# Router columns inside the first gate product, and the residual of the first layer added on TensorE

## The reference, cut to what matters

```python
x = x + xattn(ctx, layernorm(x), ...)   # selective scan over 512 positions, 16 states for each of 512 channels
x = x + ffn(layernorm(x), ...)          # router + 2 of 16 experts + one shared expert
# inside xattn, after the scan:
y = ys + D * u ; y = y * silu(z)        # z is the normalised x, turned to channels
# inside ffn:
logits = x @ gate_w.T                   # 16 router columns, softmax, top 2
gu_s = x @ shared_gate_up               # 4 * 352 columns: gate, then up
y = routed(x) + (silu(g) * u) @ shared_down
```

## Time and profile before

| | us |
|---|---|
| median of three runs (1036.51 to 1041.99) | 1039.0 |
| the profiled execution, its own time | 1039.41 |
| its span, first to last instruction | 1037.3 |
| outside the span in that execution | 2.1 |
| PE busy | 902.5 |
| DVE busy | 823.2 |
| POOL busy | 745.5 |
| ACT busy | 529.9 |
| mean granted TensorE clock, share of 2.4 GHz | 0.922 |

### The profile page before, as it was taken

One profiled execution on the slowest core, in us unless ns is written; L12 is line 12 of the kernel. 1 busy time (PEld: TensorE's weight loads), 2 busy tenths in 40 slices (PEclk: granted clock), 3 DMA queues, 4 the chain that ended last, 5 costly groups with the idle time before them and its releaser, 6 DMA issues.

```text
span 1037.3 us, 16660 instructions
## 1 busy us (share of the span) xinstructions
PE 902.5 (87%) x4352; PEld 658.6 (63%) x4353; DVE 823.2 (79%) x1348; ACT 529.9 (51%) x997; POOL 745.5 (72%) x465
## 2 busy tenths in 40 slices
PE   6787556779999889988999999889998999998994
PEld 2233245556666556655666565659988999897993
DVE  5788899999999799989999616766999979898000
ACT  3767734446665566655665322135544555454551
POOL 1436699889999899989993101148877888887873
PEclk9878765689999999999999989989998999999997
DMA  6467922563228422562210410254767767684433
GB/s 208 147 246 286 371 79 87 198 238 91 72 73 305 162 81 81 208 234 85 81 61 31 147 59 11 70 175 123 227 164 211 181 173 226 159 245 91 79 61 41
DMA packets 70260, 152.14 MB, mean 147 GB/s; under 512 B 7602, under 2 KB 24498, under 8 KB 64579
## 3 DMA queue, kind: packets, MB, share of 16 engines
q1 hardware_dynamic: 59682, 126.97, 35.3%
q0 software_dynamic: 10528, 24.65, 12.1%
HBM read 112.80 MB, written 38.80 MB: 146 GB/s over the span
## 4 chain that ended last, share of the span: by engine, by line
PE 45%; DVE 27%; issue 16%; DMA 5%; ACT 2%; POOL 2%; DVEq 1%; SPq 1%; POOLq 0%; ACTq 0%
DVE bank L1415 7%; PE bank L790 6%; PE bank L792 6%; PE bank L791 6%; PE bank L686 6%; PE bank L705 6%; DVE gs L1429 6%; PE bank L632 4%; PE bank L561 2%; DVE e_gu_lo L1578 2%; DVE e_gu_hi L1577 1%; PE bank L779 1%; DVE h_p L1415 1%; DMA xt<-x_scratch 1%; DVE p_acc L1355 1%
## 5 line engine op out<-in xcount | busy, mean ns | idle before, releaser
L1221 POOL TENSOR_TENSOR dbu<-bcs,m_w 128x2048 f32<-128x2048 f32 x64 | 296.5, 4634 | 21.4 <-DMA u_scratch<-p_u 8.5
L966 ACT ACTIVATE bank<-m_dt,c_a 128x512 f32<-128x512 f32 x256 | 171.7, 686 | 173.3 <-DVE gs L1429 173.2
L1415 DVE TENSOR_TENSOR_SCAN bank<-bank,dbu 128x512 f32<-128x512 f32 x192 | 229.9, 1217 | 11.3 <-ACT bank L966 7.4
L686 PE MATMUL bank<-ws_gu,f_xnT 128*128 128x352 f32 x576 | 192.7, 476 | 1.9 <-ACT f_hT L988 1.7
L632 PE MATMUL bank<-ident,gs 128*128 128x128 f32 x768 | 134.5, 307 | 54.8 <-DVE gs L1429 47.6
L632 PEld LDWEIGHTS bank<-ident,gs 128*128 128x128 f32 x768 | 97.9, 156 | 110.1 <-DVE gs L1429 89.1
L686 PEld LDWEIGHTS bank<-ws_gu,f_xnT 128*128 128x128 f32 x576 | 107.1, 197 | 49.4 <-issue 6.1
L790 PE MATMUL bank<-e_gu_hi,e_xT_hi 128*128 x376 | 130.0, 346 | 6.5 <-POOL e_xT_lo L1283 3.1
L1429 DVE TENSOR_TENSOR gs<-bank,bcs 128x512 f32<-128x512 f32 x192 | 127.3, 670 | 0.0
L792 PE MATMUL bank<-e_gu_hi,e_xT_lo 128*128 x376 | 122.0, 324 | 0.0
L791 PE MATMUL bank<-e_gu_lo,e_xT_hi 128*128 x376 | 121.8, 324 | 0.0
(11 more groups left out here) (175 smaller groups left out, 1692.2 us busy)
## 6 DMA issues: line engine op xcount, KB each, us to landing
bcs<-bc_scratch SPq DMA_DIRECT2D x32, 1024.0 KB, 9.1
e_gu<-in_wgu SPq DMA_DIRECT2D x16, 1408.0 KB, 9.0
e_dn<-in_wdn SPq DMA_DIRECT2D x16, 512.0 KB, 4.3
out_rows<-xt SPq DMA_DIRECT2D x18, 256.0 KB, 2.1
p_x<-in_x SPq DMA_DIRECT2D x4, 1024.0 KB, 6.8
u_scratch<-p_u SPq DMA_DIRECT2D x4, 1024.0 KB, 4.3
silu_z_scratch<-p_sz SPq DMA_DIRECT2D x4, 1024.0 KB, 5.6
dt_scratch<-p_dt SPq DMA_DIRECT2D x4, 1024.0 KB, 4.6
```

What stands on the lines that cost most here:

```text
L686: last = mm(dst[:, 0:I], lhs[t], ws_gu[:, t, off:off + I], start=t == 0, stop=t == KH - 1)
L966: f(HS[k % RING_H][:], m_dt[:, q % 2, :], ACT.Exp, scale=c_a[:, q, n:n + 1]).then_inc(exp_done, 1)
L1221: g.tensor_tensor(part_, Bs[:, gr * GRP:(gr + 1) * GRP, :], w, ALU.mult).then_inc(dbu_ready, 1)
L1415: v.tensor_tensor_scan(to, h, dbu[:, n, :], 0.0, ALU.mult, ALU.add).then_inc(scan_done, 1)
```

## The change

- `ws_gu` gets 16 more columns between the first 352 (gate, first half) and the rest, and the router's weights are loaded there; the tile `c_gate` is gone as a tile of its own. The load at L414 becomes three transfers, and one of the transfers at L371 is gone. In the slots 4 to 15, and for two tiles in the tail, the first gate product is 368 columns wide instead of 352, and ScalarE copies the 16 logits from its bank. The `router` product stays for three tiles in the tail, now one behind the other after the fourth `xn_turn`.
- `take_y` writes the gated rows to SBUF (in place of silu(z)) instead of PSUM. In slots 1 to 15 TensorE then adds them and x in bank 7 by two products with the unit matrix, 512 columns each, after the second `y_sum` of the slot; ScalarE copies the bank to `m_x` at n = 6, ahead of `gate`, and this increments `x1_ready`. `gated` on VectorE stays only once, after the last slot.

```diff
-        c_gate = sb("c_gate", [P, KH, NE])
-        ws_gu = sb("ws_gu", [P, KH, 4 * I])
+        ws_gu = sb("ws_gu", [P, KH, 4 * I + NE])
+        c_gate = ws_gu[:, :, I:I + NE]
...
+ADD_X_AT, X1_AT = 1, 6
-TAKE_AT, LOGITS_AT, GATED_AT, HIDDEN_AT, STATS_AT, ADD_AT = 2, 5, 4, (9, 13), (8, 1), 15
+TAKE_AT, LOGITS_AT, HIDDEN_AT, STATS_AT, ADD_AT = 2, 5, (9, 13), (8, 1), 15
...
+            def add_x(b, i, q, copied):
+                pe.wait_ge(y_taken, i + 1)
+                pe.wait_ge(x_loaded[q % 2], b * 32 + (q // 2) * 16 + 16)
+                pe.wait_ge(xnT_copied, 1 + copied)
+                mm(TP[:], ident[:], m_szT[:, q % 2, :], start=True, stop=False)
+                mm(TP[:], ident[:], m_x[:, q % 2].rearrange("p t j -> p (t j)"), start=False, stop=True).then_inc(x_added, 1)
...
                     dst, off, done = GU[c], half * 2 * I + c * I, (gate_ready, up_ready)[half]
+                    off += NE if off else 0
+                    wide = I + NE if with_logits and off == 0 else I
...
                             pe.wait_ge(sg_ready, 2 * f[0] + c + 1)
+                            if with_logits and c == 0:
+                                pe.wait_ge(lg_copied, 1 + f[0])
                         for t in ts:
-                            last = mm(dst[:, 0:I], lhs[t], ws_gu[:, t, off:off + I], start=t == 0, stop=t == KH - 1)
+                            last = mm(dst[:, 0:wide], lhs[t], ws_gu[:, t, off:off + wide], start=t == 0, stop=t == KH - 1)
...
-                if rows:
-                    router(f, f[0], f[0])
                 for piece in early[0:PE_AT[0]] + late[0:LATE_AT[0]]:
                     piece()
                 for n in range(NS):
                     y_sum(b, q, n)
+                    if n == ADD_X_AT and not (isinstance(i, int) and i == 0):
+                        add_x(*((b, i - 1, q - 1) if q else (b - 1, i - 1, DT - 1)), i - DT if rows else 0)
...
-            whole((first + 1, 1), first)
+            whole((first + 1, 1), None, with_logits=True)
             for q in range(TB - 1):
                 xn_turn((first + q, q), B * DT)
-                router((first + q, q), first + q + 1, first + 2)
-            whole((first + 2, 2), NT - 1)
+            whole((first + 2, 2), None, with_logits=True)
             xn_turn((NT - 1, TB - 1), B * DT)
-            router((NT - 1, TB - 1), NT, NT - 1)
-            router((NT, 0), NT, NT - 1)
+            for f in range(NT - 2, NT + 1):
+                router((f, f % TB), NT - 1)
...
+            def x1_copy(b, i, q):
+                act.wait_ge(x_added, i + 1)
+                f(m_x[:, q % 2], TP[:].rearrange("p (t j) -> p t j", t=TB), ACT.Copy).then_inc(x1_ready, 1)
...
             def lg_copy(fx):
-                act.wait_ge(lg_ready, fx[0] + 1)
-                f(logits[:, bass.ds(fx[0], 1), :].rearrange("p a e -> p (a e)"), LG, ACT.Copy).then_inc(lg_copied, 1)
+                act.wait_ge(gate_ready, 2 * (fx[0] + 1) + 1)
+                f(logits[:, bass.ds(fx[0], 1), :].rearrange("p a e -> p (a e)"), LOGITS, ACT.Copy).then_inc(lg_copied, 1)
...
                     if n == DU_AT:
                         skip(b, q)
+                    if n == X1_AT and not first:
+                        x1_copy(*((b, b * DT + q - 1, q - 1) if q else (b - 1, b * DT - 1, DT - 1)))
...
-            def take_y(b, i, q, copied):
+            def take_y(b, i, q, to):
                 dve.wait_ge(ymm_done, (i + 1) * NS)
-                dve.wait_ge(xnT_copied, 1 + copied)
                 dve.wait_ge(s_loaded[q % 2], b * 32 + (q // 2) * 16 + 16)
-                v.tensor_tensor(TP[:], Y[:], m_szT[:, q % 2, :], ALU.mult).then_inc(y_taken, 1)
+                v.tensor_tensor(to, Y[:], m_szT[:, q % 2, :], ALU.mult).then_inc(y_taken, 1)
...
                     if n == TAKE_AT and later:
-                        take_y(*((b, i - 1, q - 1) if q else (b - 1, i - 1, DT - 1)), i - DT if rows else 0)
-                    if n == GATED_AT and later:
-                        gated(*((b, i - 1, q - 1) if q else (b - 1, i - 1, DT - 1)))
+                        take_y(*((b, i - 1, q - 1) if q else (b - 1, i - 1, DT - 1)), m_szT[:, (q + 1) % 2, :])
```

More of the change, by code:

```diff
@@ L98, in program @@
         G, U = GU
-        LG = YO[:, 0:NE]
+        LG, LOGITS = YO[:, 0:NE], GU[0][:, I:I + NE]
         RANK, TOT, TABLE = bank[0], bank[3], bank[7]
@@ L264, in program @@
             gx0_loaded gx1_loaded ex_ready exT_copied eg_ready eu_ready esg_ready eh_ready ehT_ready ehT_copied
-            ey_ready ey_taken scattered tstat_done route_step idx_step waits_passed row_scaled norm_made in_rest moment_done""".split()
+            ey_ready ey_taken scattered tstat_done route_step idx_step waits_passed row_scaled norm_made in_rest moment_done x_added""".split()
         s = {n: sem(n) for n in names}
@@ L294, in program @@
         moment_done = s["moment_done"]
+        x_added = s["x_added"]
         row_scaled, norm_made, in_rest = s["row_scaled"], s["norm_made"], s["in_rest"]
@@ L413, in _ @@
             load_bc(0, 3, 1)
-            sp.dma_start(ws_gu[:], sgu.rearrange("(t p) n -> p t n", p=P)).then_inc(weights_loaded, 16)
+            sgu_rows = sgu.rearrange("(t p) n -> p t n", p=P)
+            for dst, src in ((ws_gu[:, :, 0:I], sgu_rows[:, :, 0:I]), (c_gate, gateT.rearrange("(t p) n -> p t n", p=P)),
+                             (ws_gu[:, :, I + NE:], sgu_rows[:, :, I:])):
+                sp.dma_start(dst, src).then_inc(weights_loaded, 16)
             for c in range(2):
@@ L658, in xn_turn, with router @@
                 last.then_inc(xnT_ready, 1)
-            def router(f, copied, added):
-                pe.wait_ge(xnT_copied, 1 + copied)
+            def router(f, added):
+                pe.wait_ge(xnT_copied, 1 + f[0])
                 pe.wait_ge(down_added, 1 + added)
@@ L664, in router, with shared @@
                 for t in range(KH):
-                    last = mm(LG, f_xnT[:, (f[1] + 3) % 4, t * P:(t + 1) * P], c_gate[:, t, :], start=t == 0, stop=t == KH - 1)
+                    last = mm(LG, f_xnT[:, (f[1] + 3) % 4, t * P:(t + 1) * P], ws_gu[:, t, I:I + NE], start=t == 0, stop=t == KH - 1)
                 last.then_inc(lg_ready, 1)
-            def shared(f, routed, residual=False):
+            def shared(f, routed, residual=False, with_logits=False):
                 at = (f[1] + 2) % 4
@@ L701, in down @@
                         pe.wait_ge(down_added, 1 + f[0])
-                        pe.wait_ge(lg_copied, 1 + routed)
+                        if routed is not None:
+                            pe.wait_ge(lg_copied, 1 + routed)
                     n = IT[t][1]
@@ L718, in slot @@
                     f = ((b - 1) * DT + q, q)
-                    late = shared(f, f[0] + 1, residual=True)[SPLIT:]
-                    early = shared((f[0] + 1, (q + 1) % TB), f[0] + 1)[:SPLIT]
+                    late = shared(f, None, residual=True)[SPLIT:]
+                    early = shared((f[0] + 1, (q + 1) % TB), None, with_logits=True)[:SPLIT]
                 elif q == DT - 1:
-                    early = shared((0, 0), 0)[:SPLIT]
-                if rows:
-                    router(f, f[0], f[0])
+                    early = shared((0, 0), None)[:SPLIT]
                 for piece in early[0:PE_AT[0]] + late[0:LATE_AT[0]]:
@@ L1016, in lg_copy, with lg_alone @@
             def lg_copy(fx):
-                act.wait_ge(lg_ready, fx[0] + 1)
-                f(logits[:, bass.ds(fx[0], 1), :].rearrange("p a e -> p (a e)"), LG, ACT.Copy).then_inc(lg_copied, 1)
+                act.wait_ge(gate_ready, 2 * (fx[0] + 1) + 1)
+                f(logits[:, bass.ds(fx[0], 1), :].rearrange("p a e -> p (a e)"), LOGITS, ACT.Copy).then_inc(lg_copied, 1)
+            def lg_alone(fx):
+                act.wait_ge(lg_ready, fx[0] - (NT - 2) + 1)
+                f(logits[:, fx[0], :], LG, ACT.Copy).then_inc(lg_copied, 1)
             def row_out(fx):
@@ L1081, in xnT_of @@
                 xnT_copy((first + q, q), first + q - 1)
+            lg_copy((first, 0))
             gate((first + 1, 1), 0)
@@ L1089, in _ @@
             xn_of(1)
-            lg_copy((first, 0))
             xnT_of(1)
             xn_of(2)
-            lg_copy((first + 1, 1))
             xnT_of(2)
             xn_of(3)
-            lg_copy((first + 2, 2))
+            lg_copy((first + 1, 1))
             whole((first + 2, 2))
             xnT_of(3)
-            lg_copy((NT - 1, TB - 1))
-            lg_copy((NT, 0))
+            for row in range(NT - 2, NT + 1):
+                lg_alone((row, row % TB))
             act.wait_ge(rt_max, 1)
@@ L1542, in _ @@
                     slot(b, q, True)
-            take_y(B - 1, B * DT - 1, DT - 1, NT - TB)
+            dve.wait_ge(xnT_copied, 1 + NT - TB)
+            dve.wait_ge(x1_ready, B * DT - 1)
+            take_y(B - 1, B * DT - 1, DT - 1, TP[:])
             gated(B - 1, B * DT - 1, DT - 1)
```

15 lines of the change are left out of this document (7 added, 8 removed).

## The result

The changed kernel takes 1049.7 us (median of 18 runs) where the kernel before takes 1039.9: ratio 1.0092, 95% interval 1.0074 to 1.011. That is slower by 9.7 us; the forecast was 5.5. The profiled execution took 1052.3 (span 1050.6); set against the 1039.4 of before it is at the high side, so single stages are also read in a second profile of each kernel (e8, e11).

A forecast was written before the change was run, and what follows sets the result against it. VectorE was taken to set a slot's pace, TensorE and GpSimd within about a microsecond. Terms 0.7 + 0.8 + 5.5 - 1.5 = +5.5 gave 1044.9 us (1044.5 against the median); likeliest 1042 to 1047, range 1037 to 1050.

The forecast's parts named there:

- Part 4: Slots 1 to 3: unit products at the low clock delay VectorE, +0.4, +0.4 and 0; +0.8, bounds -1.5 and +1.7.
- Part 5: First slot of later sequences: x1 ready later, +2.5 in slot 4, +2.3 in 8, +0.7 in 12; +5.5.
- Part 6: Tail: the router behind the third turn goes with its wait, partly offset by low clock; -1.5, bounds -3 and 0.
- rival (c): ScalarE stands at x_added in every slot, +0.4 in twelve slots on top: 1049; chance 0.18, shared with a longer low clock.
- longer low clock: TensorE's low clock lasts longer than the forecast had it; chance 0.18, shared with rival (c).
- Part 1: VectorE: gated goes in slots 1 to 15, 8.9 us saved if nothing else is late.
- Part 2: TensorE in second to fourth slots of a sequence: added products lose VectorE's 0.59 and 0.1 more; +0.7, bounds -0.2 and +2.
- Rival (b): In the slots TensorE has room and VectorE keeps what it saved: 1032.5, slots of 26.7; chance 0.10.
- Part 3: ScalarE in the slots: new copy of 0.49; bank ready at 407.82, ScalarE there at 407.86, even; nothing added.

The follow-up runs named there:

- e8: The kernel before, run again unchanged for a second profile; 1042.0 us in one run.
- e11: The changed kernel, run again unchanged for a second profile; 1047.6 us in one run.
- e4: The changed kernel with the unit products behind the slot's first y_sum instead of its second; 1038.8 us, 0.9981 of the kernel before.
- e6: The changed kernel with only ScalarE's bank copy moved, behind decay 7 instead of decay 6; 1045.3 us, 1.0049 of the kernel before.
- e1: The kernel before with the unit products and bank copy alone, the router's own products kept in place; 1053.2 us, 1.0112 of the kernel before.
- e7: e4 with a third unit product, its sum overwritten, ahead of the two; 1049.5 us, 1.0117 of the kernel before.
- e12: The changed kernel plus unused unit-matrix products in slots 1 and 2, six before the first y_sum, three before each other; 1041.2 us, 1.0005 of the kernel before.
- e2: The changed kernel with x1 still summed by VectorE in every slot, only the router's columns moved into the gate product; 1040.4 us, 1.0002 of the kernel before.
- e14: The kernel before with e12's filler in slots 1 and 2, as a control; 1039.1 us, 1.0008 of the kernel before.

## Why the prediction was wrong

Two steps failed. Part 4 put slots 1 to 3 at +0.8, where ScalarE, standing at `x_added`, made them +2.0 in the mean of two profiles. And the sum had no term at all for the loop's return, which came to another +2.0. Parts 5 and 6 had the right kind; the two profiles lie 1.0 and 2.4 us from the value of part 5, and 1.0 and 1.7 us from that of part 6. The time of 1049.7 is the number of the prediction's rival (c), or of its longer low clock, at a chance of 0.18. Its mechanism holds in part: ScalarE stood in six slots of fifteen, not in every one.

**Part 1 (VectorE, 8.9 saved if nothing else is late): right.** Where ScalarE doesn't stand, slots 1-3 give 1.4 (e4) and 1.8 (e6) of the 1.8 that three additions are; elsewhere others are late.

**Part 2 (+0.7 in the second to fourth slots): right**, measured +0.57 in the six steps between and -0.01 in the last. 27.40 from scan to scan in slot 10, 27.45 foretold; the router's time lost into the wait for `hT_copy` (e1), the unit products 1.72, the residual without a bracket before it. Rival (b) falls with it. The Trainium skill, in Perfetto Trace Analysis (Identifying the Most-Contended Engine), judges TensorE's headroom by the share of weight loads and by the arithmetic done, not by matmul busy time. Here that share of weight loads is 17.49 of 27.40 us, and yet a product more cost 0.86 in each of these steps (e7). The measurement decides.

**Part 3 (ScalarE even at `x_added`): right in slot 10** (418.30 + 0.20 against the copy's start at 418.50), with nothing to spare. In slots 1 to 4, 8 and 12 of the first profile ScalarE waited 1.4 to 2.4 us, as rival (c) had feared of every slot.

**Part 4 (slots 1 to 3, +0.8): the first step that failed.** Measured +2.6 and +1.5 in the two profiles. I had +0.4, +0.4 and 0: a mean between the two levels of the clock for slots 1 and 2, and nothing for slot 3, "where the second layer's products begin". The +0.7 that I had worked out for the lower clock was right: slots 1 and 2 measured +0.6 and +0.8, in the second profile +0.8 and +0.8, with a stall of VectorE in slot 2 of 1.26. In slot 3 the first profile had the gate products at the lower clock and +1.25, the second -0.12. The Trainium skill, in TensorE: Matmul & The Clock Gate (Part 1), says that activity releases the throttle. By that rule the prediction had the term near -1. The trace agrees as to the rule and not as to the term. From `take_y` to `take_y` slot 1 ran at 0.69 and 0.80 of the clock in the two profiles of the changed kernel and at 0.50 and 0.62 in those of before. But its unit products still took 3.24 us (151.21 to 154.45) and 3.41, and only the sums behind them were fast. With e12's filler the clock was 1.00, and the term -1.3.

**Part 5 (+5.5): right in kind, 0.7 low in the mean, and wrong in its picture of a fixed clock.** The turns measured +7.9 in the first profile and +4.5 in the second, so that 5.5 lies near their mean is in part luck. Slot 8 was as worked out: x1 2.3 and 2.5 later, foretold 2.3. For slots 4 and 12 I took one value each. The profiles show two: in slot 12 +0.8 with full clock (foretold 0.7) and +2.4 with the lower one; in slot 4 +0.9 and +3.2 (foretold 2.5). Which of them an execution gets differs from one to the next, and slot 8 itself had full clock in e12. (In slot 4 the lower clock is on the gate products ahead; the unit products took 1.72 in both profiles.) Two waits share the lateness, not one: the statistics' wait rose from 5.0 to 7.6 (foretold 9 to 12), the rest is VectorE behind ScalarE, as in part 4.

**Part 6 (-1.5): right on average, not in the changed kernel's own profiles.** The four profiles with the old tail have 68.0 to 69.0, the thirteen with the new one 64.5 to 68.6, mean 66.5. In the five that are over 67 the last router product is at the lower clock (1.86 us; in those at 65.2 to 65.5 it takes 1.04 to 1.22). The 0.8 us of it is not the 2 to 3 us by which these tails are longer; what else is slow there was not followed. TensorE after the last turn, for the earlier trace rows:

```profile
629.50 1.04 PE L677 MATMUL bank<-ws_gu,f_xnT 128*128 128x16 f32 x8 [0.39 <-issue]
630.90 1.04 PE L677 MATMUL bank<-ws_gu,f_xnT 128*128 128x16 f32 x8 [0.37 <-ACT logits L1042]
632.30 1.86 PE L677 MATMUL bank<-ws_gu,f_xnT 128*128 128x16 f32 x8 [0.36 <-ACT logits L1042]
```

**The return of the loop: a term that I did not have.** VectorE's two gaps there are 6.7 to 7.3 in sum in the three profiles of the kernel before and its filler version, 9.0 and 9.3 in the changed kernel's, 7.3 to 10.3 in the others. e2 has 8.5, so the router's part alone brings most of it, in that one profile; e7 has 7.3 with e4's VectorE program, where e4 has 9.4, so that program's length doesn't settle it. Both kernels' gaps ahead of slot 8 lie in a stretch in which the DMA engines are full (share 1.01 in either row above), but the shorter gap is in as full a stretch as the longer one. The Trainium skill, in Runtime: NRT & Kernel Launch (Instruction fetch mechanics), says that a taken branch out of the fetched window waits for a DMA of the target. Were VectorE's gaps such waits, they could queue with these loads. No trace here shows the fetch, and no run moved the loads, so the cause of the 2 us stays open.

In sum, to the forecast's 5.5: +1.2 in part 4, +0.7 in part 5, +1.4 in the tail as it fell out in these two profiles, +2.0 at the return, -0.1 in part 2. That is 10.7 by these rounded terms; the stretches ahead of slot 1 and behind the tail take 1.0 of it back, which I had not looked at either, and 9.7 is measured. The largest missing term is the return's; of those that the prediction had, part 4 and the tail were off by most, and the experiments show that part 4's came from ScalarE's place in line (e6) behind products that were late by the lower clock (e12) and by their own place (e4).

## What to carry to other kernels

Where work goes from an engine that keeps the pace to one that idles between sums, price it at the clock that the idling leaves, and then look at what stands in line behind its consumer. In slots 1-3 the slow products cost nothing by themselves (e6), and about 4 us of the first profile by ScalarE's wait ahead of the decays. In the six steps where TensorE was nearly full, a product costs its whole 0.86 (e7). Put such a product where its inputs first exist, not one step later; that one constant was worth 10.8 us by the medians, some 8 of it in the slots. Where an engine is within 0.3 us of being late, profile twice: two levels of the clock make two kernels of one.

## What the runs showed of the hardware that was not expected

Useless products in TensorE's waits of slots 1 and 2 took 3.4 us out of slots 1-3 of the changed kernel (e12) and left the kernel before as it was (e14): where they stand, a filler is worth what stands behind the low clock, and no more. With it, slots 1 and 2 ran at 1.00 and 0.94 of the clock in both kernels, instead of 0.69 and 0.68 in the changed one. The whole kernel came out about 9 us faster; the cause of the other 5 to 6 is open.

The level in the turns is not the same from one execution to the next. In slot 8 after, TensorE waited 2.65 and 0.99 around one sum, and then a pair of instructions took 1.91 that takes 1.02 at full clock. In e11 the waits ahead of slot 12's products were 1.57 and 0.99 and the clock stayed; in the first profile they were the same, 1.57 and 0.99, and it fell. TensorE there, e11 and then the first profile:

```profile
475.02 0.66 PE L636 MATMUL bank<-ident,gs 128*128 128x128 f32 x4 [0.99 <-DVE gs L1454]
475.52 1.02 PE L661 MATMUL bank<-m_szT,ident 128*128 128x512 f32 x2
...
474.53 0.65 PE L636 MATMUL bank<-ident,gs 128*128 128x128 f32 x4 [0.99 <-DVE gs L1454]
475.02 1.81 PE L661 MATMUL bank<-m_szT,ident 128*128 128x512 f32 x2
```
